# Summaries of the context in nine passes, sorted experts one tile deeper, context projections kept across a stage, and more drains on POOL

## The reference

```python
x = x + xattn0(layernorm(x), token_ids, ctx, ctx, ctx)
#   expert e = min(clip(id) // 6250, 3):  y = (silu(h @ ctx[e].T) * (h @ ctx[e].T)) @ ctx[e].T
x = x + ffn0(layernorm(x), norm_w, w_gv, w_out)      # rmsnorm, 8-bit rows, ternary weights
x = x + xattn1(layernorm(x), ctx, Wq, Wg, bg, Wkv, Wo)
#   k, v = split(ctx @ Wkv.T);  k = where(k > 0, k + 1, exp(k))
#   kv_summary = einsum('bhsd,bhse->bhde', k, v);  k_sum = k.sum(-2)
x = x + ffn1(layernorm(x), gate_w, w_gate, w_up, w_down, sw_gate, sw_up, sw_down)
```

## Time and profile before

| | us |
|---|---|
| runs | 1083.84, 1084.77, 1086.29 (median 1084.77) |
| profiled execution, its own time | 1083.31 |
| its span | 1081.6 |
| TensorE busy | 1039.3 (96%) |
| DVE, ACT, POOL busy | 671.2 (62%), 592.2 (55%), 284.0 (26%) |
| mean granted clock of TensorE | 0.993 |

### The profile page before, as it was taken

One profiled execution on the slowest core, in us unless ns is written; L12 is line 12 of the kernel. 1 busy time (PEld: TensorE's weight loads), 2 busy tenths in 40 slices (PEclk: granted clock), 3 DMA queues, 4 the chain that ended last, 5 costly groups with the idle time before them and its releaser, 6 DMA issues.

```text
span 1081.6 us, 16225 instructions
## 1 busy us (share of the span) xinstructions
PE 1039.3 (96%) x5830; PEld 819.7 (76%) x5830; DVE 671.2 (62%) x1226; ACT 592.2 (55%) x891; POOL 284.0 (26%) x445
## 2 busy tenths in 40 slices
PE   7999999979999999999999999999999999999994
PEld 5887877767455555578888888887888899999993
DVE  6746545527899998766565655667724566666650
ACT  5666777745898889873323234221204466666651
POOL 1012222214455544110000033100010244444442
PEclk9999999999999999999999999999999999999998
DMA  6683656530100010201111333202053687888853
GB/s 217 232 301 109 172 153 194 164 98 28 62 21 20 21 30 11 96 3 59 56 63 40 108 113 92 98 25 68 11 188 114 210 235 227 223 225 225 224 122 39
DMA packets 47607, 127.03 MB, mean 117 GB/s; under 512 B 5811, under 2 KB 6835, under 8 KB 46773
## 3 DMA queue, kind: packets, MB, share of 16 engines
q1 hardware_dynamic: 36516, 97.53, 26.9%
q0 software_dynamic: 10448, 27.58, 11.4%
q10 hardware_dynamic: 576, 1.05, 0.3%
HBM read 97.76 MB, written 28.38 MB: 117 GB/s over the span
## 4 chain that ended last, share of the span: by engine, by line
PE 70%; DVE 3%; ACT 2%; issue 1%; POOL 0%; DVEq 0%; ACTq 0%
PE bank L54 16%; PE bank L55 16%; PE bank L56 16%; PE bank L1338 10%; PE bank L1359 5%; PE bank L2157 1%; PE bank L1350 1%; PE bank L1432 1%; PE bank L1414 1%; PE bank L1443 1%; PE bank L1442 1%; PE bank L1368 1%; PE bank L2144 0%; DVE s_prod L2293 0%; DVE a_aT_l L1665 0%
## 5 line engine op out<-in xcount | busy, mean ns | idle before, releaser
L1338 PE MATMUL bank<-w,f_qT 128*128 128x512 bf16 x512 | 117.8, 379 | 1.3 <-DVE f_h L1582 1.3
L1992 POOL DMA_INDIRECT out<-e_y,scatter_idx x32 | 69.1, 2158 | 115.6 <-ACT e_y L2087 111.4
L1338 PEld LDWEIGHTS bank<-w,f_qT 128*128 128x128 bf16 x512 | 48.6, 98 | 52.4 <-issue 1.4
L1980 POOL DMA_INDIRECT e_xg<-xn_rows,gather_idx x32 | 33.7, 1054 | 167.2 <-DVE gather_idx L2335 100.7
L2029 ACT ACTIVATE s_m_h<-s_mid 128x512 fp32r<-128x512 f32 (+1 forms) x24 | 15.2, 631 | 109.4 <-DVE s_mid L2345 60.6
L54 PE MATMUL bank<-wkv_h,ctx_h_all 128*128 128x512 f32 x128 | 53.3, 417 | 12.0 <-DVE wkv_l L708 7.4
L54 PE MATMUL bank<-e_xT_h,e_wg_h 128*128 128x256 f32 (+1 forms) x192 | 56.4, 294 | 2.9 <-issue 2.1
L1359 PE MATMUL bank<-w,f_q2T 128*128 128x512 bf16 x256 | 57.9, 379 | 0.3 <-ACT f_q2T L1108 0.3
L1582 DVE SCALAR_TENSOR_TENSOR f_h<-bank,f_columns,f_sg 128x512 f32<-128x512 f32 x64 | 47.9, 749 | 12.7 <-PE bank L1338 6.2
L2435 DVE TENSOR_TENSOR e_mid<-bank,e_sil 128x256 f32<-128x256 f32 (+1 forms) x48 | 20.3, 423 | 55.5 <-ACT e_sil L2061 46.8
L55 PE MATMUL bank<-e_xT_l,e_wu_h 128*128 128x256 f32 (+1 forms) x192 | 54.1, 282 | 0.0
(11 more groups left out here) (416 smaller groups left out, 3305.0 us busy)
## 6 DMA issues: line engine op xcount, KB each, us to landing
wraw<-in_wffn SPq DMA_DIRECT2D x48, 512.0 KB, 4.3
e_raw_g<-in_ew_gate SPq DMA_DIRECT2D x16, 704.0 KB
e_raw_u<-in_ew_up SPq DMA_DIRECT2D x16, 704.0 KB
e_raw_d<-in_ew_down SPq DMA_DIRECT2D x16, 512.0 KB
sorted_y<-e_y SPq DMA_DIRECT2D x19, 256.0 KB
x_rows<-rows SPq DMA_DIRECT2D x16, 256.0 KB, 2.0
xn_rows<-a_work SPq DMA_DIRECT2D x16, 256.0 KB, 2.0
s_raw<-x_rows SPq DMA_DIRECT2D x16, 256.0 KB, 2.7
```

The costliest lines, as they stand in the source:

```text
L1338: ins = pe.matmul(bank[c % 2][:, :], qT[t % 2][:, k * P:(k + 1) * P], w_gv(k, col + c * 512), start=(k == 0), stop=(k == KD - 1))
L1980: gp.indirect_dma_start(xg[t][u][:, :], None, g.xn_dram, bass.IndirectOffsetOnAxis(g.gather_idx[:, slot:slot + 1], 0)).then_inc(e_arrived[ ...
L1992: gp.indirect_dma_start(io["out"], bass.IndirectOffsetOnAxis(g.scatter_idx[:, slot:slot + 1], 0), e_y[t][u][:, :], None, compute_op=ALU.ad ...
```

## The change

Four edits.

1. **Summaries.** v's high part, the ones and v's low part lie side by side in one tile `v_hl` (4 groups x 258 columns), and three of the four groups get a bank each (banks 4, 5, 6), where k_h x (v_h, ones, v_l) is one matmul of 258 columns. The fourth group shares bank 4 in the old form. `take_summary` adds the two halves up. Counting and sorting share bank 7.
2. **Sorted experts.** expand and turn_x of a later tile come ahead on TensorE, with silu, product, statistics, scales and fetch one tile earlier, and the tables of silu and exp loaded by dummy instructions (`first_silu`, `first_exp`). The transposes of x of tiles 0, 1 and 2 go to banks 7, 2 and 6; bank 6 holds a part of the last summary until then.
3. **Kept projections.** Three halves of the last batch's projections (keys of tile 0, values of tile 0, keys of tile 1) are computed in stage 1 into banks 0, 6 and 1, where stage 2 reads them.
4. **Drains.** POOL gets a DRAIN at the start of the last stage's `body` and in `add(14)` and `add(15)`.

```diff
@@ front_experts0
-        FETCH = 4
+        FETCH = 5
...
+        v_hl = before_w3.some(2, "v_hl", [P, KD, VW + P], f32r)
...
-        bd_bank, route_bank, sort_bank = g.bank[4:6], g.bank[6], g.bank[7]
+        bd_bank, sort_bank = g.bank[4:7], g.bank[7]
+        route_bank = sort_bank
...
+        def xbank_of(t):
+            return g.bank[2] if t == 1 else xbank[t // 2 % 2] if t < 3 else xbank[(t + 1) % 2]
@@ POOL
                 for t in range(NT):
-                    if t + 3 < NT:
-                        scales(t + 3)
+                    if t + 4 < NT:
+                        scales(t + 4)
@@ ACT
                 split_x(0)
+                act.wait_ge(s["made"], 1)
+                act.activation(first_silu[:, :], g.zeros[:, 0:1], ACT.Silu)
                 normalise(2)
                 split_x(1)
                 silu(0)
+                split_x(2)
...
+                normalise(3)
+                silu(1)
                 for t in range(NT):
                     split_mid(t)
-                    if t + 2 < NT:
-                        split_x(t + 2)
+                    if 1 <= t and t + 3 < NT:
+                        normalise(t + 3)
...
-                    if t + 1 < NT:
-                        silu(t + 1)
+                    if t + 2 < NT:
+                        silu(t + 2)
                     if t + 3 < NT:
-                        normalise(t + 3)
+                        split_x(t + 3)
...
+                act.activation(first_exp[:, :], g.zeros[:, 0:1], ACT.Exp)
@@ TensorE, summarise
+                        if c < KD - 1:
+                            out = bd_bank[c][:, 0:VW + P]
+                            pe.matmul(out, kh, v_hl[n % 2][:, c, :], start=(t == 0), stop=False)
+                            pe.matmul(out[:, 0:VW], kl, v_h[n % 2][:, c, :], start=False, stop=(t == 3 and c > 0))
@@ TensorE, turn_x
-                    if t == 1:
+                    if t == 0:
                         pe.wait_ge(s["scales_ready"], 1)
+                    if t == 2:
+                        pe.wait_ge(s["summ_ready"], BATCHES)
...
+                def kept_tile(t, half, out):
+                    for k in range(KD):
+                        mm3(pe, out[:, :], [x[:, B - 1, k * S + t * P:k * S + (t + 1) * P] for x in (g.ctx_h, g.ctx_l)],
+                            [x[:, k, half * D:(half + 1) * D] for x in (wkv_h, wkv_l)], k == 0, k == KD - 1)
@@ TensorE, the list
+                    if n == TILES - 2:
+                        total()
                     if n == TILES - 1:
-                        total()
                         turn_x(0)
                     if n:
                         summarise(n - 1)
...
+                expand(0, experts[0])
+                turn_x(2)
+                expand(1, experts[1])
                 for t in range(NT):
                     turn_mid(t)
                     if t + 2 < NT:
-                        turn_x(t + 2)
...
+                        experts.append(expert(t + 2))
+                        expand(t + 2, experts[t + 2])
+                    if t + 3 < NT:
+                        turn_x(t + 3)
+                    if t == NT - 2:
+                        pe.wait_ge(mid_ready, NT)
+                        kept_tile(0, 0, g.kept_kbank[0])
+                    if t == NT - 1:
+                        pe.wait_ge(x_lo, NT)
+                        kept_tile(0, 1, g.kept_vbank[0])
+                    contract(t, experts[t])
+                kept_tile(1, 0, g.kept_kbank[1])
@@ DVE, the list
+                    if n == TILES - 1:
+                        split_x(0)
                     if n >= TILES - 3:
                         statistics(n - TILES + 3)
...
                     if t + 2 < NT:
-                        split_x(t + 2)
+                        product(t + 2)
                     if t + 3 < NT:
-                        statistics(t + 3)
...
+                        split_x(t + 3)
+                    if t + 4 < NT:
+                        statistics(t + 4)
@@ stage 2, TensorE
+        K_KEPT, V_KEPT = 2, 1
...
-                keys_values(0)
-                for t in range(1, 4):
+                keys_values(1)
+                for t in range(2, 4):
                     keys_values(t)
-                    summarise(t - 1)
+                    summarise(t - 2)
                 turn_q(0)
+                summarise(2)
                 summarise(3)
@@ last stage, POOL
+            if e >= E1 - 2:
+                gp.drain()
             gp.sem_inc(y_free[1 - u], 1)
...
         def body():
+            gp.drain()
             gp.wait_ge(found_ready, 1)
```

More of the change, by code:

```diff
@@ L372, in split_x @@
                         act.wait_ge(a_ready, t - 1)
-                    act.activation(x_h[t % 2][:, :, :].rearrange("p k n -> p (k n)"), xbank[t % 2][:, :], ACT.Copy).then_inc(x_hi, 1)
+                    act.activation(x_h[t % 2][:, :, :].rearrange("p k n -> p (k n)"), xbank_of(t)[:, :], ACT.Copy).then_inc(x_hi, 1)
                 def silu(t):
@@ L567, in _ @@
                     if t + 2 < NT:
-                        turn_x(t + 2)
-                    if t + 1 < NT:
-                        after = expert(t + 1)
-                        expand(t + 1, after)
-                    contract(t, e)
-                    e = after
+                        experts.append(expert(t + 2))
[10 more added lines that the diff above has]
+                kept_tile(1, 0, g.kept_kbank[1])
             @block.vector
@@ L1017, in after @@
                     gp.tensor_scalar(shift2[u][:, :], mv2[u][:, 0:1], rstd2[u][:, 0:1], -1.0, ALU.mult, ALU.mult).then_inc(shift2_ready, 1)
-                for t in range(3):
-                    fetch(t)
                 for t in range(2):
@@ L1023, in _ @@
                 ins.then_inc(ones_ready, 1)
+                for t in range(3):
+                    fetch(t)
                 for t in range(3):
@@ L1300, in keys_values @@
                 def keys_values(t):
-                    for half, bank, free, ready in ((0, kbank, feature_ready, feature_in), (1, cvbank, v_lo, cv_ready)):
+                    for half, bank, free, ready, kept in ((0, kbank, feature_ready, feature_in, K_KEPT), (1, cvbank, v_lo, cv_ready, V_KEPT)):
+                        if t < kept:
+                            continue
                         if t >= 2:
```

67 lines of the change are left out of this document (38 added, 29 removed).

## The result

The changed kernel takes **1072.53 us** in the median (1072.15 to 1073.10, 4 runs), the kernel before 1085.53 over its now four runs (1083.84 to 1087.21). The ratio is 0.9882, with a 95% interval from 0.9866 to 0.9899: 13.0 us less. Forecast were 1066 and 19 us less, with a range up to 1072.5. So the sign was right, the gain came out a third smaller than forecast, and the time lies 0.03 us outside the range. The profiled execution took 1072.15 us with a span of 1070.3, against 1083.31 and 1081.6, which is 11.2 less in its own time and 11.3 in span.

What follows compares the result with a forecast made beforehand. TensorE, busy 1039.3 of 1081.6 us, was taken to bound the kernel. An FFN start 12.9 us earlier and a last drain 6.1 shorter gave -19.0, so 1083.3 became 1064.3 and the median 1066, range 1061.5 to 1072.5.

Steps and rivals of the forecast that it cites:

- What bounds the kernel: Whole kernel: TensorE, busy 1039.3 of 1081.6 us; gains only from its work, its waits, or time outside its matmuls.
- the drains: End of the program: three earlier POOL drains cut the final one from 6.59 to 0.5 us, -6.1.
- the barrier: Between stages 1 and 2: one kept half hidden, stage 2 4.4 us after contract(18), TensorE idle 1.6, clock staying full.
- the way to the FFN: Stage 2 to the FFN's first matmul: bound by DVE, 22.7 us instead of 30.1, TensorE's own work 19.8.
- Nine passes: Context summaries, nine matmuls for twelve: 0.3 us less a tile, -3.0 over ten summaries.
- The seam: Context tiles to sorted experts: TensorE waits 2.3 us at turn_x(2), but -2.7 at the same step of the work.
- The loop: Sorted experts: TensorE at its own pace, 6.44 us a tile; turn_mid(1) to contract(18)'s end takes 115.1.
- stays at 6.90: Rival for the sorted loop: ACT or a gather of over 4 us binds, 6.3 us more, 1072; chance 8%.
- gathers land late: Rival for the sorted loop: every landing takes 5.7, rounds of 7.9 us, 21 us more, 1087; chance 3%.
- The clock: TensorE: idle 2.3 us at turn_x(2) may lower the clock once, adding 1.4; counted only in the range.
- The drain in add(14): Last stage: about 60 DMAs to clear, 5.0 us, just hidden behind the scatter; otherwise costs 0 to 1.
- one costlier case: Upper end of the range, 1072.5: covers either rival at 1072, drain time not by DMA count (10%) or loop at 6.90 (8%).

Runs made afterwards that it cites:

- e8_no_kept: The changed kernel without its three kept projections in stage 1: 1075.78 us, ratio 0.9900 to the kernel before.
- e11_six_twelve: The changed kernel with six buffers for gathered rows instead of five and twelve passes for a summary instead of nine: 1071.72 us, ratio 0.9877.
- e6_before_drains: The kernel before with the three new POOL drains and nothing else: 1078.96 us, ratio 0.9940.
- e12_before_fetch5: The kernel before with its gathers five ahead instead of four, in the same five buffers: 1084.60 us, ratio 0.9995.
- e2_six_buffers: The changed kernel with six buffers for gathered rows instead of five, gathers one tile further ahead: 1068.90 us, ratio 0.9843.
- e9_small_loads: The changed kernel with seven eighths left out of each second FFN weight load during the sorted loop: 1069.33 us, ratio 0.9855.

## Why the prediction was right and wrong

**What bounds the kernel, the drains, the barrier, the way to the FFN: right.** The last drain fell by 6.4, the end came 6.2 earlier behind the last scatter, for 6.1 forecast. The barrier took 4.4, with 1.43 idle instead of 4.24 and the clock at its full level behind it (e8_no_kept shows the 4.23 without the kept half). The FFN started 22.9 after stage 2, forecast 22.7, with TensorE waiting for k_l.

**Nine passes: right, to 0.1 us** (2.9 for 3.0). The rule of the Trainium skill that was weighed there ("TensorE: Matmul & The Clock Gate", section "Back-to-back issue gap") would have had nothing of it, or an estimated 2.4 with its figure for streams. The run e11_six_twelve, with 2.9, is on the side of the trace's 0.112 a pass. That project(11) still ended 0.5 late has another source. The wait for wtot was 0.3 for the 0.4 forecast, but TensorE also waits 1.1 for ctx_l_all at 15.71. The profiled execution of the kernel before doesn't have this wait, while others with its code there do (0.73 in e6_before_drains, 0.58 in e12_before_fetch5), so it differs between executions and is no part of the change.

**The seam: right by 0.3.** The wait at turn_x(2) was 2.67 for 2.3.

**The loop: wrong, and this is the step that failed.** "Both under 6.44, so TensorE runs at its own pace" held a round of 5.8, made with the median landing of 3.6, against the pace. The round itself, from gather to gather, was the right one: 145.47 to 153.48 is 8.0 us with a landing of 5.7, and the price of the rival had 7.9 for it. Wrong was the landing in it: 3.6, the median of the kernel before, for every tile. Landings went up to 5.9, and the longest gave rounds of 8.0 and 8.2 (from 166.10 to 174.31). TensorE is the bound, so it never makes up for a late tile, and an average says nothing; the sum of the excesses counts. So the term of 115.1 us, from turn_mid(1) to the last contraction's end, measured 119.4. At +4.2 us this was a case of the rival "stays at 6.90" in its size (6.3) with the mechanism of the rival "gathers land late", whose price of 21 had taken the slowest landing for all of them. e2_six_buffers gives the 4.2 back (4.7 at stage 2), e9_small_loads names the weights' loads as the larger part of what the gathers meet.

**The clock: a term left out of the sum, and the second step that failed.** An idle time ahead of the last summary was forecast (22.7 for 19.8), and at the seam such a one was said to cost perhaps 1.4; here it was not counted. It cost 1.7, of which 1.1 behind the FFN's start. The 1.5 us at 471 are of this kind too, and no part of the change; they are the luck of this execution.

**The drain in add(14): hidden otherwise than I argued.** The scatter before it landed 6.5 us after its issue and not 5.1, so the drain ended at 1051.5, and the next scatter went at 1052.20, some 2 us late by the rhythm of before. It cost nothing, since the two scatters of expert 15 came when they did before: from 1040.00 to the last issue it is 22.94 us, in the kernel before 22.85 from the same scatter (1045.23). The drain in add(15) had 2 DMAs to clear and not 4, and took 0.20.

**The range** had its upper end at the price of one costlier case. The loop (4.2) and two drops of the clock (2.6 behind the FFN's start) came together. That the time is just 0.03 outside says little either way: the forecast missed the gain by 6 us.

## What to carry to other kernels

A producer with a ring of buffers has a deadline for each item: from what lets its transfer be issued (here POOL's scales for the item before) to the need of the item, the slowest transfer must fit, not the median one, and a kernel bound by one engine pays in full each miss that reaches this engine. Where a loop is made faster, look for transfers that were hidden by its slack, and for bulk loads that run in the same microseconds. Ask of preparation work on several engines in turn which of it the next matmul really needs, and whether the part that is moved back has an in-order engine (here POOL) that then comes too late.

## What of the hardware was not expected

- A drain of POOL takes its time by the DMAs that POOL issued since the last one: 2 in 0.20, 25 in 2.28, 60 in 4.95, 80 in 6.59 us, and 16 in 2.68, of which 1.3 was an operation still running. The counts are those of the program. That is 0.08 to 0.10 us each; a fixed cost as large as the 0.33 of the forecast isn't there (it would make the first 0.49).
- The clock of TensorE fell behind idle times of 1.3 to 2.7 us in some executions and not in others, with the same code there (0.51 and 1.00, 0.53 and 1.00 in the rows above). Behind the wait for k_l ahead of the last summary, of 1.10 to 3.03 us, it fell each time.
- Gathers of 256 KB that landed in 3.4 us, in the median, with small loads beside them took up to 5.9 beside loads of 512 KB (3.9 in the median). One with small loads beside it still took 5.3; what that one met no run shows.
